# GRU scan with block attention: order of the first transfers and the path of the constants

## What is computed

```python
def cell(h, x):
    gi = x @ W_ih + b_ih
    gh = h @ W_hh + b_hh
    r, z = sigmoid(i_r + h_r), sigmoid(i_z + h_z)
    n = tanh(i_n + r * h_n)
    return (1 - z) * n + z * h
x = x + scan(cell, cond, x)                  # [32, 64, 512]
block_repr = x.reshape(B, 8, 8, 512).sum(axis=2)
keys = rmsnorm(block_repr @ Wk.T) * rms_weight
attn = softmax(keys @ cond[1])               # over the 8 blocks
y = x + (attn @ block_repr) @ Wo.T
out = x + layernorm(y) * gamma + beta
```

## Time and profile before

| what | us |
|---|---|
| median of 3 runs | 384.88 |
| the three runs | 381.39 to 385.06 |
| the profiled execution | 382.3 |
| its span, first to last instruction | 380.5 |
| its mean granted TensorE clock | 0.991 |

### The profile page before, as it was taken

How to read it: one execution, slowest core, us unless ns; L and a number is a source line. 1 busy time by engine, 2 the same in 40 slices (tenths; PEclk the granted TensorE clock), 3 DMA queues, 4 the chain that set the end, 5 groups by cost and what they waited for, 6 DMA issues and landing times.

```text
span 380.5 us, 9825 instructions
## 1 busy us (share of the span) xinstructions
PE 363.2 (95%) x3281; PEld 213.9 (56%) x3281; DVE 261.8 (69%) x1134; ACT 159.3 (42%) x506; POOL 20.2 (5%) x53
## 2 busy tenths in 40 slices
PE   7999999999999999999999999999999999996873
PEld 4466555566666555556666655556666654334552
DVE  2735667687676767786768676867777676778675
ACT  4712326262625343434435262626262556582300
POOL 7011000000000000000000000000000001000120
PEclk9999999999999999999999999999999999999898
DMA  5975535423232323232232414142323222101056
GB/s 180 399 287 118 163 88 162 115 51 97 72 97 69 97 69 95 70 73 72 69 96 56 109 46 106 35 114 50 97 69 97 69 69 72 29 28 29 3 203 239
DMA packets 27484, 38.63 MB, mean 102 GB/s; under 512 B 2988, under 2 KB 19016, under 8 KB 27464
## 3 DMA queue, kind: packets, MB, share of 16 engines
q1 hardware_dynamic: 27432, 38.36, 34.8%
q10 hardware_dynamic: 32, 0.01, 0.0%
HBM read 18.17 MB, written 4.19 MB: 59 GB/s over the span
## 4 chain that ended last, share of the span: by engine, by line
PE 89%; DVE 5%; issue 2%; DMA 1%; POOL 1%; SPq 1%; POOLq 0%; ACT 0%; DVEq 0%
PE gates_ps L595 42%; PE gi_ps L563 36%; DMA h_tok<-hist 1%; DVE gcx L1090 1%; PE first_ps L595 1%; PE first_ps L656 1%; PE fourth_ps L595 1%; PE third_ps L595 1%; PE keys_ps L595 1%; PE fourth_ps L656 1%; PE third_ps L656 1%; PE keys_ps L656 1%; POOL w_hh L367 1%; PE gi_ps L577 0%; PE keys_ps L721 0%
## 5 line engine op out<-in xcount | busy, mean ns | idle before, releaser
L595 PE MATMUL gates_ps<-w_hh,turned 128*32 128x384 f32 x1920 | 167.3, 489 | 0.5 <-DVE turned L808 0.5
L595 PEld LDWEIGHTS gates_ps<-w_hh,turned 128*32 128x32 f32 x1920 | 56.4, 109 | 85.6 <-issue 56.4
L563 PE MATMUL gi_ps<-w_ih_hi,xt_hi 128*128 128x384 f32 x240 | 87.2, 363 | 0.0
L563 PE MATMUL gi_ps<-w_ih_hi,xt_lo 128*128 128x384 f32 x240 | 81.2, 338 | 0.0
L563 PE MATMUL gi_ps<-w_ih_lo,xt_hi 128*128 128x384 f32 x240 | 80.2, 334 | 0.0
L477 ACT ACTIVATE rz<-gates_ps 128x256 f32<-128x256 f32 x60 | 23.1, 385 | 128.9 <-PE gates_ps L595 128.8
L870 DVE TENSOR_TENSOR rz<-gates_ps,rz 128x128 f32<-128x128 f32 x60 | 17.5, 292 | 80.4 <-ACT rz L477 80.4
L563 PEld LDWEIGHTS gi_ps<-w_ih_hi,xt_hi 128*128 128x128 f32 x240 | 45.0, 187 | 37.5 <-issue 37.5
L563 PEld LDWEIGHTS gi_ps<-w_ih_lo,xt_hi 128*128 128x128 f32 x240 | 45.1, 188 | 0.0
L563 PEld LDWEIGHTS gi_ps<-w_ih_hi,xt_lo 128*128 128x128 f32 x240 | 45.0, 187 | 0.0
L808 DVE STREAM_TRANSPOSE turned<-hist 128x32 f32<-128x32 f32 (+1 forms) x192 | 36.7, 217 | 2.2
(11 more groups left out here) (218 smaller groups left out, 302.1 us busy)
## 6 DMA issues: line engine op xcount, KB each, us to landing
gi<-gi_tok SPq DMA_DIRECT2D x60, 192.0 KB, 3.4
x1t<-in_x_t_dram SPq DMA_DIRECT2D x16, 256.0 KB, 3.2
gcx<-in_x_tok_dram SPq DMA_DIRECT2D x16, 256.0 KB, 3.2
h_tok<-hist SPq DMA_DIRECT2D x64, 64.0 KB, 2.2
out_dram<-gcx SPq DMA_DIRECT2D x16, 256.0 KB, 2.1
gcx<-in_w_ih_dram SPq DMA_DIRECT2D x4, 768.0 KB, 8.0
w_hh<-in_w_hh_dram SPq DMA_DIRECT2D x4, 768.0 KB, 8.5
wo_t<-in_wo_t_dram SPq DMA_DIRECT2D x1, 1024.0 KB, 5.4
```

Of the source, the lines that this page charges most:

```text
L563: mm = pe.matmul(gi_ps[tok][:, 0:G3], a[:, k, :], w[:, k, gi_cols(j)], start=(k == 0 and a is xt_hi and w is w_ih_hi), stop=(k == NJ - 1 a ...
L595: mm = pe.matmul(gates_bank(t)[j * B:(j + 1) * B, P:], before[:, k * B:(k + 1) * B], chunk(w_hh, k, j), start=False, stop=(k == NJ - 1), s ...
```

## The change

- SP issues x of the first quad and W_ih's first quarter as its very first transfers, with no wait ahead of them. The three bias rows go out on ScalarE's queue, behind the wait for `bias_made`.
- The constants no longer pass `const_rows` and TensorE. Seven broadcast transfers on SP's queue in block 0 (`load_consts`) write them into their final tiles: beta at s == 0, gamma (256 KB) at s == 1, gamma and rms_weight in recurrence layout at s == 2 and 3 (64 KB each), the query row in recurrence layout and rms_weight (256 KB) at s == 4, the query row for all partitions (256 KB in pieces of 512 bytes) at s == 6. wo_t moves from s == 3 to s == 5.
- GpSimd multiplies rms_weight by the query row (two products) before its loop. Its memset and mask for `pick` go.
- TensorE loses L642, both `lay_pick`, and two fillers ahead of the bias product; it has three fillers behind it in place of one.
- ScalarE loses the copies to `recs`, `gamma_tok` and `wq`; VectorE loses one memset and the product of the rows, and makes `beta_t` at s == 3 instead of s == 0.

```diff
@@ SP @@
+            def load_consts(s):
+                by_rec, by_j = [NJ, B, P], "(j u) -> j u"
+                q_rows = cond_d.rearrange("(j b) u -> j b u", j=NJ)
+                if s == 0:
+                    sp.dma_start(recs[:, 1, :], beta_d.rearrange(by_j, j=NJ)[:, None, :].broadcast_to(by_rec)
+                                 ).then_inc(beta_in, 16)
+                if s == 1:
+                    sp.dma_start(gamma_tok[:], gamma_d[None, :].broadcast_to([P, D])).then_inc(gamma_in, 16)
...
+                if s == 4:
+                    sp.dma_start(q_rec, q_rows[:, 1, :][:, None, :].broadcast_to(by_rec)).then_inc(consts_in, 16)
+                    sp.dma_start(wq[:], rms_d[None, :].broadcast_to([P, D])).then_inc(consts_in, 16)
+                if s == 6:
+                    sp.dma_start(q_tok.rearrange("p (j u) -> p j u", j=NJ),
+                                 cond_d.rearrange("(j b) u -> b j u", j=NJ)[1:2].broadcast_to([P, NJ, P])
+                                 ).then_inc(consts_in, 16)
+
             def steps(i, first=False, last=False):
+                if last:
+                    sp.wait_ge(wq_ready, 2)
                 for s in range(S):
-                    if first and s == 3:
+                    if first:
+                        load_consts(s)
+                    if first and s == 5:
                         sp.dma_start(wo_t[:], wo_t_d.rearrange("(k p) n -> p k n", p=P)).then_inc(wo_in, 16)
...
-            sp.wait_ge(bias_made, 1)
-            sp.dma_start(bias_rows[0:NJ, 0:G3], b_ih_d).then_inc(bias_in, 16)
...
             sp.dma_start(x1t[:, 0], x_t_d[:, 0:NJ, :]).then_inc(x_first_in, 16)
             load_w_ih(0)
@@ GpSimd @@
             pool.memset(own_rows, 0.0).then_inc(pick_made, 1)
-            pool.memset(pick, 0.0).then_inc(pick_made, 1)
...
+            pool.wait_ge(consts_in, 16 * 5)
+            pool.tensor_tensor(wq[:], wq[:], q_tok, ALU.mult).then_inc(wq_ready, 1)
+            pool.tensor_tensor(wq_rec, wq_rec, q_rec, ALU.mult).then_inc(wq_ready, 1)
             pool.wait_ge(b_in_ready, NJ)
+            pool.wait_ge(wq_ready, 2)
@@ ScalarE @@
-            act.wait_ge(rows_made, 1)
-            for c, row in enumerate((gamma_d.rearrange("(j u) -> j u", j=NJ), beta_d.rearrange("(j u) -> j u", j=NJ),
...
+            act.wait_ge(bias_made, 1)
+            act.dma_start(bias_rows[0:NJ, 0:G3], b_ih_d).then_inc(bias_in, 16)
...
-                if k == 0:
-                    act.wait_ge(consts_laid, 1)
-                    act.activation(recs[:].rearrange("p c u -> p (c u)"), gi_ps[0][:, 0:3 * P], ACT.Copy
-                                   ).then_inc(consts_kept, 1)
-                    act.wait_ge(consts_laid, 2)
-                    act.activation(gamma_tok[:], gi_ps[1][:], ACT.Copy).then_inc(consts_kept, 1)
...
-                if peeled and s == 0:
-                    act.wait_ge(consts_laid, 3)
-                    act.activation(wq[:], small_ps[:], ACT.Copy).then_inc(consts_kept, 1)
+                if peeled and s == S - 1:
                     act.wait_ge(beta_turned, 1)
@@ TensorE @@
-                if first and s == 0:
-                    lay_pick(small_ps, 2)
...
-            keep_warm(2)
-            pe.wait_ge(pick_made, 4)
+            pe.wait_ge(pick_made, 3)
             pe.wait_ge(bias_in, 48)
             pe.matmul(first_ps[0][:], own_rows, bias_rows, start=True, stop=True).then_inc(bias_laid, 1)
-            pe.wait_ge(pick_made, 5)
-            pe.wait_ge(wq_row_ready, 1)
-            pe.matmul(gi_ps[0][:, 0:3 * P], own_rows, const_rows[:, 0:3, :], start=True, stop=True
-                      ).then_inc(consts_laid, 1)
-            lay_pick(gi_ps[1], 0)
-            keep_warm(1).then_inc(pe_warmed, 1)
+            keep_warm(3).then_inc(pe_warmed, 1)
...
@@ VectorE @@
-                if peeled and s == 0:
-                    dve.wait_ge(consts_kept, 2)
+                if peeled and s == 3:
+                    dve.wait_ge(beta_in, 16)
                     dve.transpose(beta_t[:], beta_rec).then_inc(beta_turned, 1)
...
+                if peeled and s == S - 1:
+                    dve.wait_ge(gamma_in, 16)
...
-            dve.memset(const_rows, 0.0).then_inc(rows_made, 1)
             dve.memset(bias_rows, 0.0).then_inc(bias_made, 1)
```

More of the change, by code:

```diff
@@ L100, in gru_block_attention @@
         own_rows, zeros = gcx[:, 14, 0:P], gcx[:, 14, P:2 * P]
-        pick = gcx[:, 15, :].rearrange("p (j m) -> p j m", j=NJ)
-        const_rows = h_tok[:].rearrange("p (c u) -> p c u", u=P)
+        q_tok, q_rec = gcx[:, 15, :], gcx[:, 14, 2 * P:3 * P]
         b_hh_rz = gi[:, 0, 0:2 * D].rearrange("p (j n) -> p j n", j=NJ)
@@ L115, in gru_block_attention @@
         w_hh_in = [sem(f"w_hh_in{k}") for k in range(NJ)]
-        bias_in, rows_in, wk_in, wo_in, h0_in, b_in_loaded, x_first_in = (
-            sem("bias_in"), sem("rows_in"), sem("wk_in"), sem("wo_in"), sem("h0_in"), sem("b_in_loaded"),
+        bias_in, consts_in, wk_in, wo_in, h0_in, b_in_loaded, x_first_in = (
+            sem("bias_in"), sem("consts_in"), sem("wk_in"), sem("wo_in"), sem("h0_in"), sem("b_in_loaded"),
             sem("x_first_in"))
@@ L120, in gru_block_attention @@
         gi_moved = [sem("gi_moved0"), sem("gi_moved1")]
-        zeros_made, bias_made, rows_made, made, pick_made = (
-            sem("zeros_made"), sem("bias_made"), sem("rows_made"), sem("made"), sem("pick_made"))
+        zeros_made, bias_made, made, pick_made = (
+            sem("zeros_made"), sem("bias_made"), sem("made"), sem("pick_made"))
         warmed, pe_warmed, bias_laid, bias_kept, first_seeded = (
             sem("warmed"), sem("pe_warmed"), sem("bias_laid"), sem("bias_kept"), sem("first_seeded"))
-        wq_row_ready, consts_laid, consts_kept, beta_turned, gmask_made, step_made = (
-            sem("wq_row_ready"), sem("consts_laid"), sem("consts_kept"), sem("beta_turned"), sem("gmask_made"),
+        wq_ready, beta_in, gamma_in, beta_turned, gmask_made, step_made = (
+            sem("wq_ready"), sem("beta_in"), sem("gamma_in"), sem("beta_turned"), sem("gmask_made"),
             sem("step_made"))
@@ L228, in move_h @@
                              ).then_inc(h_tok_in, 16)
+            def load_consts(s):
[6 more added lines that the diff above has]
+                    sp.dma_start(gamma_tok[:], gamma_d[None, :].broadcast_to([P, D])).then_inc(gamma_in, 16)
+                if s == 2:
+                    sp.dma_start(recs[:, 0, :], gamma_d.rearrange(by_j, j=NJ)[:, None, :].broadcast_to(by_rec)
+                                 ).then_inc(consts_in, 16)
+                if s == 3:
+                    sp.dma_start(recs[:, 2, :], rms_d.rearrange(by_j, j=NJ)[:, None, :].broadcast_to(by_rec)
+                                 ).then_inc(consts_in, 16)
+                if s == 4:
[4 more added lines that the diff above has]
+                                 cond_d.rearrange("(j b) u -> b j u", j=NJ)[1:2].broadcast_to([P, NJ, P])
+                                 ).then_inc(consts_in, 16)
             def steps(i, first=False, last=False):
+                if last:
+                    sp.wait_ge(wq_ready, 2)
                 for s in range(S):
-                    if first and s == 3:
+                    if first:
+                        load_consts(s)
+                    if first and s == 5:
                         sp.dma_start(wo_t[:], wo_t_d.rearrange("(k p) n -> p k n", p=P)).then_inc(wo_in, 16)
@@ L306, in _ @@
             pool.memset(own_rows, 0.0).then_inc(pick_made, 1)
-            pool.memset(pick, 0.0).then_inc(pick_made, 1)
             own = own_rows.rearrange("p (j b) -> p j b", j=NJ)
             for half_ in range(2):
-                pool.wait_ge(pick_made, 2 + half_)
+                pool.wait_ge(pick_made, 1 + half_)
                 pool.affine_select(out=own, in_=own, compare_op=ALU.not_equal, fill=1.0, base=-NJ * half_,
                                    pattern=[[-1, NJ], [0, B]], channel_multiplier=1).then_inc(pick_made, 1)
-            pool.affine_select(out=pick, in_=pick, compare_op=ALU.not_equal, fill=1.0, base=0,
-                               pattern=[[-1, NJ], [0, P]], channel_multiplier=1).then_inc(pick_made, 1)
             pool.memset(ident[:], 0.0).then_inc(made, 1)
@@ L376, in split_x @@
                 act.activation(xt_hi[:], x1t_of(quad), ACT.Copy).then_inc(x_hi_ready, 1)
-            act.wait_ge(rows_made, 1)
-            for c, row in enumerate((gamma_d.rearrange("(j u) -> j u", j=NJ), beta_d.rearrange("(j u) -> j u", j=NJ),
-                                     rms_d.rearrange("(j u) -> j u", j=NJ),
-                                     cond_d.rearrange("(j b) u -> j b u", j=NJ)[:, 1, :])):
-                act.dma_start(const_rows[0:NJ, c, :], row).then_inc(rows_in, 16)
+            act.wait_ge(bias_made, 1)
+            act.dma_start(bias_rows[0:NJ, 0:G3], b_ih_d).then_inc(bias_in, 16)
```

(9 more changed lines are left out.)

2 lines of the change are left out of this document (removed).

## The result

| kernel | median us | range us | ratio to before, 95% interval |
|---|---|---|---|
| before | 384.24 (4 runs) | 381.39 to 385.06 | |
| changed | 389.12 (4 runs) | 388.17 to 391.1 | 1.0147 [1.0077, 1.0217] |

The changed kernel is slower by 1.5% by the ratio; the two medians differ by 4.9 us, which is 1.3%. Its profiled execution took 389.8 us with a span of 388.0, 7.5 us more than the profiled one before (382.3 and 380.5).

The account below looks back on a forecast made before the run. TensorE was taken to bound the kernel. Gains of 1.55 (prologue), 0.04 (step 0) and 0.89 (`lay_pick`), less 0.3 for the clock, made 2.2 us: 383.6 - 2.2 = 381.4 us, range 378.5 to 384.3.

Parts of the forecast that it names:

- What bounds the kernel: Whole chain: TensorE for 89%, steps of 5.02 us; only the prologue, TensorE's own work or first-block waits change the time.
- The transfers on SP: Prologue: everything on SP's queue is earlier by 2.4 us, with x issued at about 0.85.
- The bias under load: Prologue: bias rows on ScalarE's queue land at 4.6, between 3.95 and 5.7; the first chunk starts 1.55 us earlier.
- rival (a): Prologue: bias waits for W_ih's first quarter, landing at 5.7; gain 0.1 to 1.4 us, 382.2 to 383.5; chance 0.18.
- My own sum: Whole kernel: 1.55 + 0.04 + 0.89 - 0.3 = 2.2 us gained.
- The clock: Prologue: TensorE's pause may leave groups of L656 at the low pace; 0.3 us lost, 1.3 at worst.
- `lay_pick` in step 0: Between step 0's input chunk and step 1: its removal from TensorE gains 0.89 us in full.
- The transfers in block 0 at no cost: First block: seven broadcast transfers, some 1 MB, stand in idle time of SP's queue and cost nothing.
- The 0.65 us that I gave for a move 1 us late: First block: cost if the next quad's gi move, behind q_tok and x_tok, were 1 us late.
- GpSimd's products, beta's transpose: First block: products, some 1.8 us, run in GpSimd's idle time; the transpose is one short instruction at s == 3.
- the slower one: Prologue: bias rows queue behind all SP has issued; 6.2 us lost, 389.8; chance 0.06.

Follow-up runs that it names:

- e14_fillers: e3_wo_s3_q_2k with eight more filler products ahead of the bias product; 383.55 us, 1.0014 of before.
- e2_q_2k: Changed kernel with q_tok read in 128 pieces of 2 KB from neighbouring rows instead of 512 of 512 bytes; 386.94 us, 1.0112 of before.
- e3_wo_s3_q_2k: Changed kernel with wo_t back at s == 3 and q_tok read in 128 pieces of 2 KB; 383.36 us, 1.0008 of before.
- e1_wo_s3: Changed kernel with wo_t issued at s == 3 again; 389.43 us, 1.0183 of before.
- e9_q_own_rows: Changed kernel with wo_t at s == 3 and q_tok read as 512 pieces at different addresses (rows of x); one run, 383.71 us.
- e12_scratch: Changed kernel, bias rows on SP between x and W_ih, wo_t at s == 3, wq at s == 5, query row via 2 KB of DRAM; 380.99 us, 0.9943.
- e11_final: Changed kernel, bias rows on SP between x and W_ih, wo_t at s == 3, wq at s == 5, query row spread from one partition; 387.78 us, 1.0142.
- e5_hold: Changed kernel with SP waiting for the bias rows before it issues W_ih's second quarter; 391.25 us, 1.0192 of before.
- e4_bias_sp: Changed kernel with the three bias rows on SP's queue ahead of x again; 388.17 us, 1.0154 of before.

## Why the prediction was wrong

- **What bounds the kernel**: right. TensorE's chain at 5.02 us a step, and only the prologue and a wait in block 0 could move the time; both did.
- **The transfers on SP**: right. x went out at 0.74, and W_hh's first two quarters, which wait for W_ih's first two, at 5.63 and 8.96 (W_ih was forecast to land at 5.6 and 9.5).
- **The bias under load**: wrong, the first step that failed. I took a landing at 4.6 with 5.7 as the upper end, from cond landing with the weight quarter ahead of it. It landed at 7.2. The upper end assumed that the row waits for what was issued ahead of it; with more issued behind, it waited longer. The rule of turns by packets (the Trainium skill, DMA: Bandwidth & Descriptors, Queues, rings and completion order) allows what came out: the bias landed between W_ih's first quarter (5.6) and its second (8.9), so before SP's queue was empty but after more than the quarter ahead. The size of a turn no run here shows. This is the mechanism of rival (a), priced too low: (a) still left a gain of at least 0.1 us, and step 1 came 1.36 us late. My own sum, with the landing at 7.2 and the clock term below as measured, gives -1.3: its form was right and these two terms were not.
- **The clock**: the term was mis-sized. I took 0.3 us for groups of L656 at the slow pace; the first two took 1.45 + 1.05 us for 2 x 0.65, so 1.2 us, four times as much. The pause was 3.4 us, not 0.7. My pause followed from my landing, so one wrong term made the other: the chunk came 3.8 us after my 18.4, 2.6 by the landing and 1.2 by the pace. The slow pace as a whole was worth 1.9 us by e14_fillers; most of the rest is the bias product (2.05 against 1.11 us), which I had counted at a slow pace in both kernels.
- **`lay_pick` in step 0**: right. 0.89 forecast; step 0 to step 1 went from 5.93 to 5.06.
- **The transfers in block 0 at no cost**: wrong, the second step that failed, and the larger one: 6.9 of the 8.2 us at step 9. I saw that the move of step 8 has only 0.35 us to spare and that q_tok and x_tok stand ahead of it by 4 us, and called that enough since 3.4 us is what a move took. That is the landing time of a 192 KB move and says nothing of q_tok, for which I had no row; it took 10.5 us. I did not bound it from both sides, as I did with the bias, and I counted wo_t's new place as a relief for step 4 only, without what is late next: with wo_t at s == 5 it, wq, x and q_tok are outstanding together (e2_q_2k). The 0.65 us that I gave for a move 1 us late missed both its size (4.2 us) and the slow pace behind it (2.6 us).
- **GpSimd's products, beta's transpose**: no cost shows; e3_wo_s3_q_2k has them all, and no step of its first block waits.
- **The rivals**: the slower one was the wrong mechanism (the bias starved behind everything, 389.8). The number is near the result by chance.

What stays open: why the same 512 bytes are read so slowly; and what makes the part behind the third last step last 49.6 us in one execution and 52.9 in another, which also holds the 0.7 us between +8.2 at step 9 and +7.5 at the end of the span.

## What to carry to other kernels

A transfer put ahead of one with little to spare needs a price of its own kind: size, pieces and how often the same bytes are read, not the landing time of its neighbour. Late data can cost more than the wait when TensorE is the bound: an idle stretch of 4.2 us was followed by a step at half pace, which cost 2.6 us on top; one of 3.2 us was not. A small transfer that everything waits for goes ahead of the large ones on the same queue; on another queue it shares the engines with all that is issued until it lands.

## What the runs showed of the hardware

- 512 reads of 512 bytes from only four rows of DRAM: the core's DMA engines moved 40 GB/s at a busy share of 0.17 for six us (e1_wo_s3). 512 pieces from 512 addresses, with x_tok behind them: 238 GB/s at 0.97 (e9_q_own_rows, one run). 128 reads of the same 2 KB of DRAM: landed in 3.75 (e12_scratch) and 3.9 us (e3_wo_s3_q_2k). 128 reads of one SBUF partition's 2 KB: 37 GB/s at a share of 0.94 (e11_final).
- A 2 KB transfer on ScalarE's queue took 4.73 us with 3.6 MB issued on SP's by then or right after, 3.29 with 1.1 MB (e5_hold), 1.47 with hardly any.
- TensorE idle for 3.2 us (e2_q_2k) kept its pace, 2.79 us for the gates behind. Idle for 4.2 us (changed kernel) the gates took 5.35, for about 4.6 us in e4_bias_sp 4.13 and in e5_hold 4.48, for 6.9 us in e11_final 4.08. How slow the step behind is does not follow the length of the pause alone.
- VectorE's 128x32 additions and products took up to 0.72 us instead of 0.19 while GpSimd added 128x256 tiles (e14_fillers; e5_hold too). In the same stretch of e14_fillers those of VectorE's operations that read a PSUM bank took no longer than in the kernel before: 0.29 us for 128x128, 0.34 for two of 128x32. The sum starts when its own data land, 2 us earlier in the changed kernel than before (25.57 against 27.54); in the two runs it met VectorE's work of step 0.
